# Asking for the expert weights of a fused attention and expert kernel one batch earlier, and splitting three experts on GpSimd in quarters

## The reference

```
x = x + (softmax(q k^T / 8) v) Wproj + bproj      q = layernorm(x) Wq,  k, v = context Wkv,  16 heads of 64
x = x + sum over the 2 best of 8 experts: share * (silu(h Wg) * (h Wu)) Wd      h = layernorm(x)
```

## Time and profile before

| | |
|---|---|
| median of 3 runs | 1486.23 us (1484.23 to 1487.73) |
| the profiled execution's own time | 1491.06 us |
| its span (first to last instruction) | 1489.3 us |
| busy: PE, DVE, ACT, POOL | 97%, 69%, 55%, 37% of the span |
| mean granted clock of TensorE | 0.991 |

### The profile page before, as it was taken

How to read it: one execution, slowest core, us unless ns; L and a number is a source line. 1 busy time by engine, 2 the same in 40 slices (tenths; PEclk the granted TensorE clock), 3 DMA queues, 4 the chain that set the end, 5 groups by cost and what they waited for, 6 DMA issues and landing times.

```text
span 1489.3 us, 38380 instructions
## 1 busy us (share of the span) xinstructions
PE 1443.4 (97%) x12134; PEld 1284.8 (86%) x12135; DVE 1025.9 (69%) x2664; ACT 812.4 (55%) x2159; POOL 552.1 (37%) x641
## 2 busy tenths in 40 slices
PE   6999999999999999999999999999997899999996
PEld 5898889998888888888888998888886688888885
DVE  5667777677767677677777777777667676666664
ACT  4555555555555555555555555555555565555553
POOL 3524344343434343434343343434336243323232
PEclk9999999999999999999999999999999899999998
DMA  9222222222222222322222222213018133233332
GB/s 263 79 67 68 74 72 74 66 75 66 72 69 76 66 86 76 96 73 66 72 66 79 67 72 69 72 38 105 29 37 312 38 66 57 50 57 51 55 56 26
DMA packets 101107, 113.82 MB, mean 76 GB/s; under 512 B 17244, under 2 KB 88140, under 8 KB 101068
## 3 DMA queue, kind: packets, MB, share of 16 engines
q1 hardware_dynamic: 87900, 94.33, 21.2%
q0 software_dynamic: 12144, 15.66, 5.8%
q10 hardware_dynamic: 1024, 3.34, 0.7%
HBM read 61.37 MB, written 51.93 MB: 76 GB/s over the span
## 4 chain that ended last, share of the span: by engine, by line
PE 91%; DMA 4%; DVE 3%; issue 1%; ACT 1%; SPq 0%; POOLq 0%; DVEq 0%; ACTq 0%
PE bank L1414 25%; PE bank L1357 21%; PE bank L1483 11%; PE bank L1459 11%; PE bank L1449 9%; PE bank L1504 6%; PE bank L1421 4%; DMA out<-y_out,dest_now 2%; PE bank L1663 1%; DMA Wgu<-in_L_ffn_gate_up_w 1%; PE bank L1616 1%; PE bank L1531 1%; DMA WqL_whole<-in_L_xattn_Wq 1%; DVE probT L1215 1%; PE bank L1521 0%
## 5 line engine op out<-in xcount | busy, mean ns | idle before, releaser
L851 ACT ACTIVATE prob<-bank,neg_max 112x375 f32<-112x375 f32 x512 | 299.0, 589 | 134.0 <-DVE neg_max L1209 134.0
L1209 DVE TENSOR_REDUCE neg_max<-bank 112x1 f32<-112x375 f32 x512 | 243.7, 538 | 14.4 <-PE bank L1449 14.3
L1459 PE MATMUL bank<-ident,prob 112*125 112x112 f32 x1536 | 214.5, 273 | 2.7 <-ACT prob L851 2.4
L1459 PEld LDWEIGHTS bank<-ident,prob 112*125 112x125 f32 x1536 | 195.9, 188 | 13.9 <-ACT prob L851 5.0
L1483 PE MATMUL bank<-probT,V 125*64 125x112 f32 x3072 | 175.5, 263 | 3.0 <-DVE probT L1215 2.2
L997 DVE TENSOR_TENSOR K_l<-bank,K_h 128x376 fp32r<-128x376 f32 x256 | 140.3, 549 | 52.0 <-ACT K_h L811 45.5
L1483 PEld LDWEIGHTS bank<-probT,V 125*64 125x64 f32 x3072 | 148.1, 137 | 29.4 <-issue 26.2
L786 POOL DMA_INDIRECT out<-y_out,dest_now x63 | 97.8, 1553 | 201.2 <-DMA out<-y_out,dest_now 137.5
L1357 PE MATMUL bank<-Wgu,hT_h 128*128 x504 | 167.2, 413 | 3.9 <-DVE hT_l L1275 3.7
L987 DVE COPY V<-bank 125x512 f32<-125x512 f32 x96 | 66.4, 692 | 139.3 <-PE bank L1421 136.3
L809 ACT COPY V<-bank 125x512 f32<-125x512 f32 x96 | 56.4, 588 | 181.9 <-PE bank L1421 179.4
(11 more groups left out here) (209 smaller groups left out, 3865.1 us busy)
## 6 DMA issues: line engine op xcount, KB each, us to landing
bins<-pad_rows SPq DMA_DIRECT2D x29, 1032.0 KB, 5.8
inv_rows<-sums SPq DMA_DIRECT2D x126, 128.0 KB, 2.9
h_in<-bins SPq DMA_DIRECT2D x63, 129.0 KB, 2.3
Wgu<-in_L_ffn_gate_up_w SPq DMA_DIRECT2D x6, 1024.0 KB, 7.0
y_sb<-in_ctx SPq DMA_DIRECT2D x32, 187.5 KB, 2.7
y_sb<-in_ctx SPq DMA_DIRECT2D x62, 93.8 KB, 2.7
x_sb<-in_x SPq DMA_DIRECT2D x16, 224.0 KB, 2.9
x_res<-in_x SPq DMA_DIRECT2D x32, 112.0 KB, 2.4
```

The source lines that it names most:

```text
L851: nc.scalar.activation(prob[:, j, :], S_ps[j][0:LQ, 0:LKV], ACT.Exp, bias=neg_max[:, j:j + 1], accum_out=row_sum[:, head // HB, head % HB: ...
L1209: nc.vector.tensor_reduce(neg_max[:, j:j + 1], S_ps[j][0:LQ, 0:LKV], AX.X, ALU.max, negate=True).then_inc(max_done, 1)
L1459: last = nc.tensor.transpose(S_ps[j][0:KR, t * LQ:t * LQ + LQ], prob[:, j, t * KR:t * KR + KR], ident[0:LQ, 0:LQ])
```

## The change

SP's orders move. In batch 30, after the first `spread_inverses` and the store of batch 29, SP asks for experts 1 and 2; after the second `spread_inverses` it waits for the last value of `made`, asks for expert 3 and then for the 3 MB of second weights. Only then does it come to batch 31, whose first order is `x_res`. POOL now splits experts 0, 1 and 2, each in four quarters of 128 x 512 numbers: expert 0 early in batch 30 (behind `x_bias` of batch 30), expert 1 at the end of batch 30, expert 2 in batch 31 behind `x_bias` of batch 31 and in front of `split_O` of the first half. ACT rounds expert 3 in step 1 of batch 31 and nothing in step 2. The last `split_O` goes from POOL to ACT (rounding) and DVE (subtraction). ACT then rounds experts 4 and 5, the rows of tiles 0 and 1, and experts 6 and 7. DVE subtracts expert 3, the last O, expert 4, the rows of tiles 0 and 1, and experts 5, 6 and 7.

```diff
@@ SP, pair(i), for odd in (0, 1): after x_res and prefill
-                    if known(i) and i == NP - 1 and odd:
+                    if there(b, B):
+                        spread_inverses(b, 0)
+                    if there(b - 1, B):
+                        sp.wait_ge(x2_done, b)
+                        sp.dma_start(dram_at(tokens, b - 1), x2[:, 1 - odd, :]).then_inc(x2_out[1 - odd], 16)
+                    if known(i) and i == NP - 1 and not odd:
                         sp.wait_ge(made, a.made(a.find(0, "q", 7)))
                         load_expert(sp, 1)
                         sp.wait_ge(made, a.made(a.find(0, "K", HP - 1)))
                         load_expert(sp, 2)
+                    if there(b, B) and not (known(b) and b == B - 1):
+                        spread_inverses(b, 1)
+                    if known(i) and i == NP - 1 and not odd:
                         sp.wait_ge(made, a.n0 + len(a.items))
                         load_expert(sp, 3)
-                    if there(b, B):
-                        spread_inverses(b, 0)
-                    if known(i) and i == NP - 1 and odd:
                         sp.dma_start(Wd[:, early:E].rearrange("p e k n -> p (e k) n"),
                                      down_w[early:E].rearrange("e (k p) n -> p (e k) n", p=P)).then_inc(wd_in, 16)
-                    if there(b - 1, B):
-                        sp.wait_ge(x2_done, b)
-                        sp.dma_start(dram_at(tokens, b - 1), x2[:, 1 - odd, :]).then_inc(x2_out[1 - odd], 16)
-                    if there(b, B) and not (known(b) and b == B - 1):
-                        spread_inverses(b, 1)
@@ POOL, split_expert(e)
-                pool.tensor_copy(Wgu[:, e, 0], Wgu[:, e, 1].bitcast(F32)).then_inc(wgu_hi0, 1)
-                pool.wait_ge(wgu_hi0, e + 1)
-                lo_of_expert(e)
+                for q in range(4):
+                    hi, lo = (Wgu[:, e, part, q // 2, q % 2 * FF:q % 2 * FF + FF] for part in range(2))
+                    pool.tensor_copy(hi, lo.bitcast(F32)).then_inc(wgu_hi0, 1)
+                    pool.wait_ge(wgu_hi0, 4 * e + q + 1)
+                    if q == 3:
+                        pool.wait_ge(wgu_lo0, 3 * e + 3)
+                    pool.tensor_tensor(lo, lo.bitcast(F32), hi.bitcast(F32), ALU.subtract).then_inc(*(
+                        (wgu_ready, 1) if q == 3 else (wgu_lo0, 1)))
@@ POOL, pair(i)
-                    if known(i) and i == NP - 1 and odd:
-                        split_expert(1)
+                    if known(i) and i == NP - 1:
+                        split_expert(2 * odd)
...
                     if known(i) and i == NP - 1 and not odd:
-                        split_expert(0)
+                        split_expert(1)
             over_pairs(pool, pair, 2, tail=False)
-            split_O(2 * B - 1, 1, B - 1)
@@ ACT, pair(i)
-                        if known(i) and i == NP - 1 and odd and s in (1, 2):
-                            hi_of_experts(s + 1, s + 2)
+                        if known(i) and i == NP - 1 and odd and s == 1:
+                            hi_of_experts(3, 4)
@@ ACT, after the pairs
+            act.wait_ge(O_done, 2 * B)
+            nc.scalar.copy(OT_h[:, HALF:NJ, :].rearrange("p j q -> p (j q)"), O_now[:]).then_inc(OT_hi, 1)
             open_gates(B - 2, A_ps[1])
-            hi_of_experts(4, 7)
+            hi_of_experts(4, 6)
             for t in range(2):
                 hi_of_rows(t, t)
-            hi_of_experts(7, E)
+            hi_of_experts(6, E)
@@ DVE, after the pairs
-            for e in (2, 3, 4, 5):
-                lo_of_expert(e)
+            lo_of_expert(3)
+            dve.wait_ge(OT_hi, 2 * B)
+            nc.vector.tensor_tensor(OT_l[:, HALF:NJ, :].rearrange("p j q -> p (j q)"), O_now[:],
+                                    OT_h[:, HALF:NJ, :].rearrange("p j q -> p (j q)").bitcast(F32),
+                                    ALU.subtract).then_inc(OT_lo, 1)
+            lo_of_expert(4)
             for t in range(2):
                 lo_of_rows(t, t)
                 keep_dest(t, 0, t)
-            for e in (6, 7):
+            for e in (5, 6, 7):
                 lo_of_expert(e)
```

More of the change, by code:

```diff
@@ L410, in attention_and_experts @@
         wgu_hi, wgu_hi0, wgu_ready = sem("wgu_hi"), sem("wgu_hi0"), sem("wgu_ready")
+        wgu_lo0 = sem("wgu_lo0")
         dest_done = sem("dest_done")
@@ L668, in scatter @@
                                             hn[:, slot, k, :], None).then_inc(scattered[slot], 16)
-            def lo_of_expert(e):
-                pool.tensor_tensor(Wgu[:, e, 1], Wgu[:, e, 1].bitcast(F32), Wgu[:, e, 0].bitcast(F32),
-                                   ALU.subtract).then_inc(wgu_ready, 1)
             def split_expert(e):
                 pool.wait_ge(wgu_raw[e], 16)
-                pool.tensor_copy(Wgu[:, e, 0], Wgu[:, e, 1].bitcast(F32)).then_inc(wgu_hi0, 1)
-                pool.wait_ge(wgu_hi0, e + 1)
-                lo_of_expert(e)
+                for q in range(4):
[6 more added lines that the diff above has]
+                        (wgu_ready, 1) if q == 3 else (wgu_lo0, 1)))
             def split_O(n, half, b):
@@ L1080, in lo_of_expert @@
             def lo_of_expert(e):
-                dve.wait_ge(wgu_hi, e - 1)
+                dve.wait_ge(wgu_hi, e - 2)
                 dve.wait_ge(wgu_ready, e)
```

## The result

The changed kernel takes 1496.28 us (median of 4 runs, 1495.53 to 1496.99), the kernel before 1486.72 us (4 runs, 1484.23 to 1487.73). The ratio is 1.0071, with a 95% interval from 1.0059 to 1.0083: slower by about 10 us. I had forecast 1490.2 us, with a range from 1481 to 1496; the result lies 0.3 us above its upper end.

What follows compares the result with a forecast made beforehand. TensorE carried 91% of the chain, so only the places where the chain leaves it could move. The terms -10.1 + 12.6 + 1.5 = +4.0 us on a median of 1486.23 gave 1490.2 us, range 1481 to 1496.

Steps and rivals of the forecast that it cites:

- What would show it: Signs in batch 31: late `x_bias`, `normalise` some 9 us later, `turn_hn` released by POOL, 5.65 us stop gone, DVE-released gate.
- 12.6 + 1.5: Loss in batch 31: `turn_hn` 12.6 us late through POOL waiting for `x_res`, plus 1.5 us for TensorE's lower clock.
- the whole argument hangs on this: On SP's queue a small transfer behind a large one lands when the large one has landed.
- the long transfer: Rival: SP held in the issue of `x_res`, the 3 MB take 16.3 us, landing at 1141.8; 1494.7 us, chance 0.15.
- my own case: Main forecast: expert 3 and the 3 MB landed by 1137.3, `x_res` about then; 1490.2 us, chance 0.45.
- gain of 10.1 us: Start of the tiles: gate of tile 2 at 1160.3 and not 1170.40, as experts 4 to 7 come sooner.
- the mark: The gate product of tile 2, which waits for all eight experts; what it moves by, the end moves by.
- what then sets the mark: After `normalise` of the last half, DVE's list of subtractions, 16.2 us, sets the gate of tile 2.
- The removed stop of 5.65 us: TensorE's wait before the last projection, for the last `split_O` on POOL; expected to be gone.
- The clock: After standing some 10 us in batch 31 TensorE runs at the lower clock: 1.5 us lost, bounds 0 and 3.
- The gain without the loss: Rival: SP's queue does not hold back `x_res` and the inverses; -10.1 us, 1476.1 us, chance 0.18.
- The cancelling case: Rival: the 4 MB arrive at the fast bound, 1135.5, and the clock costs nothing; +0.7 us, 1486.9 us, chance 0.22.

Runs made afterwards that it cites:

- e2: The changed kernel with the 3 MB of second weights put back behind the first inverses of batch 31: 1487.90 us, ratio 1.0011 to the kernel before.
- e3: The changed kernel with expert 3 and the 3 MB asked for on ACT's queue instead of SP's: 1493.31 us, ratio 1.0044 to the kernel before.
- e4: The changed kernel with `x_res` of batch 31 ahead of expert 3 and the 3 MB behind the first inverses: 1488.04 us, ratio 1.0009.
- c0: The kernel before, unchanged, run again for a second profile: 1486.51 us, ratio 1.0001.
- e10: As e5, with experts 6 and 7 asked for by SP behind the rows of tiles 0 to 2, the last 1.5 MB behind them: 1490.49 us.
- e6: The kernel before with only the last `split_O` moved from POOL to ACT and DVE, no transfer moved: 1486.63 us, ratio 1.0001.
- e1: The changed kernel with only `x_res` of batch 31 asked for ahead of expert 3 and the 3 MB: 1494.75 us, ratio 1.0058 to the kernel before.
- e5: As e4, with the second weights in two halves, the later 1.5 MB behind the first tiles' rows: 1486.88 us, ratio 1.0004.
- e11: As e4, with experts 6 and 7 asked for by SP behind the rows of tiles 0 to 2: 1486.91 us, ratio 1.0003.
- e7: The changed kernel with POOL's experts split whole, not in quarters: 1496.00 us, ratio 1.0059 to the kernel before.

## Why the prediction was wrong

Every sign listed under "What would show it" came, and the number was off all the same.

**The loss was right in cause and near in size.** Counted from S, N came 13.4 us later than in the first profile and 12.9 later than in the second, against the 12.6 + 1.5 forecast. The run is 1.2 us late against the profile of before at S; without that, `x_res` landed at 1138.2 (forecast 1137.3), `turn_hn` ran at 1151.0 (1150.2), the first `normalise` at 1140.8 (1141.4). e2 shows that the cause is the 3 MB. The one thing amiss is the reason, "the whole argument hangs on this": e3 shows that a small transfer is also late when the large one stands on another queue. That SP would be held in the issue of `x_res`, the long transfer's mark, came true with 7.28 us, but the 4 MB landed as in my own case, so it cost nothing of its own.

**The step that failed is the sum, in its gain of 10.1 us.** Measured, the gain behind `normalise` was 2.6 us (21.4 against 18.8). And with the loss taken out, as in e4, no gain was left at all: 1.5 us slower than before, with an interval of the ratio from 1.0 to 1.0019. Two things were wrong with it:

First, *it was counted from a bad stretch and then set on a good median*. The profiled execution took 1491.06 us and the median of the runs 1486.23. I saw the difference, 4.8 us, and took it off at the end, as if it lay anywhere in the run. But 4.4 us of it lay in the very stretch from which I read the gain (58.3 us from S to G against 53.9 in the second profile, where the later expert's transfer took 12.6 us and not 16.9; how well the 4.4 are known is said under c0). So they were counted twice, once as a gain and once in the median. The forecast for the mark by itself, 62.3 us from S, was within 1.9 of the 64.2 measured. Against the second profile it is 8.4 us of loss, and 1486.2 + 8.4 = 1494.6.

Second, *"what then sets the mark" left a path out*. DVE's list was to take 16.2 us and its parts came as I said: 2.29 and 2.28 us for an expert, 0.62 for the last O. But it took 18.8: before the rows of tile 0 and tile 1 DVE stood 1.99 and 0.76 us for ACT, which stood for TensorE, which stood for `h_in`. The prediction named "if an unblocked queue turns out not to bring experts 4 to 7 in time" as a danger. They came in time, in about 6 us each, and in coming they made the rows late. e4 shows this path as the whole chain; in e10, where the rows are asked for after experts 4 and 5 have landed and ahead of 6 and 7, they take a third of the time.

Together: 4.4 + 1.9 is 6.3, where the 1.9 are the 2.6 us by which DVE's list was too short less the 0.7 by which the loss was too large; the forecast was 6.1 us too low. The sum closes better than its parts are known.

**The removed stop of 5.65 us was worth nothing that the runs can tell** (e6). In the first profile the stop ended at 1150.55, five microseconds before the expert landed; it couldn't have set the mark, and my sum put no price on it by itself. But it was part of the picture in which the start of the tiles had slack to take out.

**The clock.** After standing 10 us TensorE came back at the lower level: `weigh` of step 2 took 2.51 us, where the chain of the second profile of before has 1.37 for the same 24 products. From 1155 to 1160, behind the wait for POOL, the granted clock was 0.50 again (length, busy PE, PEld, DVE, ACT, POOL, granted clock, DMA share, GB/s):

```profile
1155.00:1160.00 5.00, 4.99 (x37) 4.43 (x37) 4.01 (x11) 1.48 (x4) 1.16 (x1) 0.50 0.45 168
```

But the term of 1.5 us came to nothing. From `turn_hn` to N it is 6.48 us in the changed kernel, 6.45 and 6.74 in the two profiles of before, and ahead of `turn_hn` TensorE waited 2.87 us for POOL in any case. So the whole loss is the late `turn_hn`: counted from S it ran 13.2 to 13.4 us later than before, against the 12.6 forecast. Where POOL doesn't hold TensorE, the clock's price shows: in e1 and e3 it is 13.3 us from the first `normalise` of batch 31 to N, against 11.7 and 12.0 in the profiles of before.

**The rivals.** The gain without the loss was wrong at its root. The cancelling case made the loss small; it was the gain that was small. The time came out above that of the long transfer, 1494.7, and not by its mechanism: its nearness is luck.

**Shown and not shown.** Shown by runs: the 3 MB are 8.4 of the 10 us; 7 of them are lost too when the load stands on the other queue; the parts that were to gain bring nothing once the loss is out (e4, e6); the small transfers in front of the tiles are three times as long beside the experts. Seen at the marks, but not clear of the noise in the medians: the 1.5 us of `x_res` alone (e1) and the 1.4 us of the queue (e3 against e1). Only argued: that the 4.4 us of the first profile are chance, for which there are two profiles, both of executions above their median, and the agreement of the medians with the second to 1 or 2 us. Open: the price of the quarters, what an ACT that doesn't wait for all second weights would bring, and what makes 16 KB take 6.8 us beside another queue's load.

## What to carry to other kernels

A gain read off one profiled execution belongs to that execution. Where it differs from the median by as much as the effect, look first whether the difference lies in the very stretch that is to be changed, and take a second profile. When large loads are moved earlier, list the small transfers that will be in flight with them on any queue, not only those behind them on their own: each took three times as long here. And when a stop is removed, or a load comes sooner, follow every path into the mark to its transfer; here four versions (e4, e5, e6, e11) that each removed another wait reached the mark within 0.6 us of one another.

## What the runs showed of the hardware

**The issue of a small transfer is held behind a large one.** SP stood 7.28 us in the issue of `x_res` behind 3 MB in rows of 1 KB, 3.92 us in that of the sums in e1, 4.95 us in the earlier trace rows, and 0.46 us behind an expert of 1 MB alone (e2). The same sums issued by SP while ACT's queue had the load went out in 0.57 us (e3). In every run with the 3 MB on SP's queue the held issue was over 6.0 to 8.6 us after the 3 MB had been asked for. So a long issue in the profile points to a large order ahead of it on its queue, before any landing does.

**Small transfers suffer from other queues' large ones.** The 16 KB of the sums took 6.8 us for 2.0, the 129 KB of a tile's rows 5.9 to 6.6 for 2.1, POOL's scatter of batch 29 5.6 to 6.6 where a scatter in the changed kernel took 3.5 (median of two).

**POOL's subtractions hold some of DVE's operations.** While POOL subtracted a quarter, two operations of DVE with both inputs in SBUF took as long as what was left of POOL's. With 16 and 224 columns they took 1.15 and 1.47 us in the changed kernel, and 0.17 and 0.39 in the second profile of before, where POOL had only operations on one column and, from 1138.97, `hn`. Both ended within 0.3 us of the end of a POOL subtraction (1145.92 and 1147.82). In e7, under one POOL subtraction of 4.51 us, the first of them took 0.89 us and ended 0.03 us behind it, at 1145.98. But operations of DVE that read a PSUM bank ran under the same subtraction as fast as ever (`normalise` 0.62 us, `residual` 0.41), so it isn't all of DVE that is held. The other direction is known from the earlier trace rows. DVE, after and in the second profile of before:

```profile
1144.79 1.15 DVE L1135 TENSOR_TENSOR picked<-onehot,bin_at 112x16 f32<-112x16 f32 x1
...
1146.59 1.47 DVE L1155 TENSOR_TENSOR t_cmp<-less,iota_tile 128x224 f32<-128x224 f32 x1
```

```profile
1138.07 0.17 DVE L1132 TENSOR_TENSOR picked<-onehot,bin_at 112x16 f32<-112x16 f32 x1
...
1138.76 0.39 DVE L1152 TENSOR_TENSOR t_cmp<-less,iota_tile 128x224 f32<-128x224 f32 x1
```
